# Strided cross-attention on Trainium2: three context pieces multiplied ahead of the first tokens, the second of them loaded at the first expert stage's end

## The reference

```python
Q = (hidden_states @ Wq.T + bq)          # 8 x 100 x 512, from the normalised x
K = (key_value_states @ Wk.T + bk)       # from the context
V = (key_value_states @ Wv.T + bv)
idx = jnp.arange(H)[:, None] + stride * jnp.arange(m)[None, :]   # head h: rows h, h+16, ...
scores = jnp.einsum('bhqd,bhkd->bhqk', Q, Kg) * scaling          # Kg, Vg: K, V at idx
out = softmax(scores) @ Vg, then @ Wo.T + bo
x = x + tanh(g_xattn[1]) * out
```

## Time and profile before

| | us |
|---|---|
| median of 3 runs | 2059.59 (2058.01 to 2061.52) |
| profiled execution | 2049.21 |
| its span, first to last instruction | 2047.5 |
| PE / DVE / ACT / POOL busy in the span | 1892.9 / 1043.0 / 801.4 / 641.8 |
| mean granted TensorE clock | 0.964 of full |

### The profile page before, as it was taken

One profiled execution on the slowest core, in us unless ns is written; L12 is line 12 of the kernel. 1 busy time (PEld: TensorE's weight loads), 2 busy tenths in 40 slices (PEclk: granted clock), 3 DMA queues, 4 the chain that ended last, 5 costly groups with the idle time before them and its releaser, 6 DMA issues. The chain is left out here.

```text
span 2047.5 us, 35305 instructions
## 1 busy us (share of the span) xinstructions
PE 1892.9 (92%) x12136; PEld 1542.4 (75%) x12136; DVE 1043.0 (51%) x2405; ACT 801.4 (39%) x1728; POOL 641.8 (31%) x522
## 2 busy tenths in 40 slices
PE   5799999999999999999589999999997876999994
PEld 3588788787878787878468888888875656999983
DVE  5616465565656565645553333233335755554564
ACT  3324243333434343433343334233313534555650
POOL 1220110302020202000045554355520204787872
PEclk9899999999999999999789999999998977999997
DMA  8730213122121112010333333133368034545546
GB/s 289 237 104 30 75 38 72 46 60 58 54 63 54 30 54 59 9 26 10 105 119 109 113 113 123 54 105 110 116 210 283 13 129 136 182 163 165 204 150 207
DMA packets 131587, 218.85 MB, mean 107 GB/s; under 512 B 46075, under 2 KB 50971, under 8 KB 130671
## 3 DMA queue, kind: packets, MB, share of 16 engines
q1 hardware_dynamic: 126431, 200.46, 30.6%
q0 software_dynamic: 5008, 16.48, 2.4%
HBM read 188.87 MB, written 28.04 MB: 106 GB/s over the span
## 5 line engine op out<-in xcount | busy, mean ns | idle before, releaser
L492 POOL TENSOR_TENSOR a_cols<-a_cols,a_moments_b 128x722 f32<-128x722 f32 x32 | 56.6, 1768 | 545.3 <-DMA a_moments_b<-a_moments_dram 545.3
L634 PE MATMUL a_kv_ps<-a_kvin_hi,a_wk_hi 128*128 128x512 f32 (+1 forms) x512 | 195.5, 382 | 0.0
L1098 PE MATMUL f_banks<-f_wab_hi,f_x_hi 128*128 x448 | 183.6, 410 | 2.6 <-DVE f_x_lo L1785 1.4
L635 PE MATMUL a_kv_ps<-a_kvin_lo,a_wk_hi 128*128 128x512 f32 (+1 forms) x512 | 179.7, 351 | 0.0
L636 PE MATMUL a_kv_ps<-a_kvin_hi,a_wk_lo 128*128 128x512 f32 (+1 forms) x512 | 179.6, 351 | 0.0
L1100 PE MATMUL f_banks<-f_wab_hi,f_x_lo 128*128 x448 | 176.3, 394 | 0.0
L1099 PE MATMUL f_banks<-f_wab_lo,f_x_hi 128*128 x448 | 175.8, 392 | 0.0
L568 ACT ACTIVATE a_probs<-a_probs,a_neg_max 100x822 f32<-100x822 f32 x128 | 125.9, 984 | 115.1 <-DVE a_neg_max L916 115.1
L1807 DVE TENSOR_TENSOR f_h_sb<-f_h_sb,f_banks 128x256 f32<-128x256 f32 x112 | 47.2, 421 | 239.9 <-ACT f_h_sb L1530 237.6
L634 PE MATMUL a_kv_ps<-a_wv_hi,a_kvin_hi 128*128 128x512 f32 (+1 forms) x384 | 157.0, 409 | 2.3 <-DVE a_k_lo L909 2.2
L1530 ACT ACTIVATE f_h_sb<-f_banks 128x256 f32<-128x256 f32 x112 | 43.1, 385 | 292.8 <-PE f_banks L1100 283.9
(11 more groups left out here) (419 smaller groups left out, 4786.1 us busy)
## 6 DMA issues: line engine op xcount, KB each, us to landing
f_raw<-f_pieces SPq DMA_DIRECT2D x94, 256.0 KB, 2.7
m_raw<-m_pieces SPq DMA_DIRECT2D x92, 256.0 KB, 2.9
f_wab_raw<-f_pieces SPq DMA_DIRECT2D x42, 512.0 KB, 5.9
m_wab_raw<-m_pieces SPq DMA_DIRECT2D x42, 512.0 KB, 6.0
a_cols<-ctx_cols SPq DMA_DIRECT2D x8, 1444.0 KB, 7.5
a_rows<-ctx SPq DMA_DIRECT2D x8, 1280.0 KB
ahead_piece<-g_ctx SPq DMA_DIRECT2D x2, 2880.0 KB, 20.7
a_moments_b<-a_moments_dram SPq DMA_DIRECT2D x7, 722.0 KB
```

The lines of the kernel that those rows point to most:

```text
L634: nc.tensor.matmul(out, hi_l, hi_r, start=first, stop=False)
L635: nc.tensor.matmul(out, hi_l, lo_r, start=False, stop=False)
L1098: nc.tensor.matmul(out, left_hi, right_hi, start=start, stop=False)
```

## The change

SP issues piece 1 right behind `load_stream`, at the first expert stage's end, and not behind y half 0; piece 2 takes piece 1's place in the attention's list, and piece 3 stands alone behind y half 1. PE multiplies pieces 0, 1 and 2 before the first tokens, and piece 3 between half(0) and tokens(4). The banks are dealt out in the new order. ACT's order follows: keys and values of 0, keys 1, deviations(0), values 1, keys 2, deviations(1), values 2, tokens 0 to 3, query weights, queries 0 to 3, deviations(2), keys and values 3, tokens 4 to 7, queries 4 to 7. DVE's and POOL's orders stay.

```diff
--- before.py
+++ after.py
@@ -1398,6 +1398,7 @@
                     ahead.load_values(sp)
                     ahead.load_piece(sp, 0)
                     handed.load_stream(sp)
+                    ahead.load_piece(sp, 1)
                 else:
                     sp.wait_ge(y_scattered, 16 * SLOTS)
             with sp.Else():
@@ -2083,9 +2085,9 @@
         ROUTED = 3
         GROUPS = ((0, 1, 2, 3), (4, 5), (6, 7))
         bank_use = {}
-        for kind, n in (("k", 0), ("v", 0), *(("x", b) for b in range(HB)), ("k", 1), ("v", 1), *(("q", m) for m in range(KD)),
-                        ("k", 2), ("v", 2), *(("x", b) for b in range(HB, B)), *(("q", m) for m in range(KD, 2 * KD)),
-                        ("k", 3), ("v", 3)):
+        for kind, n in (*((kind, c) for c in range(3) for kind in "kv"), *(("x", b) for b in range(HB)),
+                        *(("q", m) for m in range(KD)), ("k", 3), ("v", 3),
+                        *(("x", b) for b in range(HB, B)), *(("q", m) for m in range(KD, 2 * KD))):
             bank_use[kind, n] = len(bank_use)
         BANK_USES = len(bank_use) // 4
         assert len(bank_use) % 4 == 0
@@ -2107,10 +2109,9 @@
             sp.wait_ge(sums.tail_done, 1)
             sp.wait_ge(sums.scattered, 16 * sums.core)
             sums.load_half(sp, 0)
-            ahead.load_piece(sp, 1)
+            ahead.load_piece(sp, 2)
             sp.dma_start(wq_raw[:, :, :], wq_t).then_inc(wq_loaded, 16)
             sums.load_half(sp, 1)
-            ahead.load_piece(sp, 2)
             ahead.load_piece(sp, 3)
             sp.wait_ge(mid_done, B)
             sp.dma_start(wo_raw[:, :, :], wo_t).then_inc(wo_loaded, 16)
@@ -2181,24 +2182,26 @@
                                      scale=SCALE).then_inc(fill_free("q", n), 1)
 
             act.wait_ge(zero_k, 1)
+            act.wait_ge(const_done, 2)
             move_keys(0)
             move_values(0)
-            act.wait_ge(const_done, 2)
-            for g in range(2):
-                deviations(g)
-                for b in EQUAL[g]:
-                    move_tokens(b)
+            move_keys(1)
+            deviations(0)
+            move_values(1)
+            move_keys(2)
+            deviations(1)
+            move_values(2)
+            for b in range(HB):
+                move_tokens(b)
             act.wait_ge(wq_loaded, 16)
             for k in range(KD):
                 nc.scalar.activation(wq_hi[:, k, :], wq_raw[:, k, :], ACT.Copy).then_inc(wq_hi_done, 1)
-            move_keys(1)
-            move_values(1)
             act.wait_ge(q_bias_done, 1)
             for n in range(KD):
                 move_queries(n)
             deviations(2)
-            move_keys(2)
-            move_values(2)
+            move_keys(3)
+            move_values(3)
             for b in range(HB, B):
                 move_tokens(b)
             def high_output_weights(k):
@@ -2210,8 +2213,6 @@
                 move_queries(n)
                 if n >= KD + 2:
                     high_output_weights(n - KD - 2)
-            move_keys(3)
-            move_values(3)
             for k in range(2, KD):
                 high_output_weights(k)
             act.wait_ge(c_loaded, 32)
@@ -2310,18 +2311,17 @@
                 for n in range(KD * h, KD * h + KD):
                     queries(n)
 
-            context(0)
+            for c in range(3):
+                context(c)
             pe.wait_ge(const_done, 3)
             for b in range(HB):
                 tokens(b)
-            context(1)
             pe.wait_ge(wq_lo_done, KD)
             half(0)
-            context(2)
+            context(3)
             for b in range(HB, B):
                 tokens(b)
             half(1)
-            context(3)
 
             def element(b):
                 if b >= 4:
```

## The result

| us | before | changed |
|---|---|---|
| median, 20 runs of each | 2056.71 (2046.34 to 2061.98) | 2061.66 (2055.74 to 2067.89) |
| profiled execution | 2049.21 | 2055.74 |
| its span | 2047.5 | 2054.0 |
| PE / DVE / ACT / POOL busy | 1892.9 / 1043.0 / 801.4 / 641.8 | 1895.5 / 1046.0 / 801.9 / 642.3 |
| mean granted TensorE clock | 0.964 | 0.963 |

The ratio of the times, run against run, is 1.0025 (95% interval 1.0013 to 1.0037): the changed kernel is slower by about 5 us, a quarter of a per cent.

The account below looks back on a forecast made before the run. PE was taken as bound by waits for tokens, sequences, piece 2 and DVE, plus low-clock stretches. Half(0) at 1569.1 + 30.3 + 3.3 = 1602.7 against 1598.65, +4.0 on 2059.6: 2063.6 us, range 2057.0 to 2067.5.

Parts of the forecast that it names:

- Step 1: At the expert stage's end, piece 1's early transfer makes the last scatters wait, delaying SP's release by 4.0 us.
- the estimate by equal turns: For the scatters beside piece 1: queues sharing engines equally from 1525 on would make the delay nearer 3 us than 4.
- The room: Idle DMA engine time between 1526 and 1536, at share 0.65: 3.5 us of piece 1's 7.1 fit in.
- up to another microsecond of the room isn't usable: In SP's delay: the idle stretch's end lies behind the last scatter's data, so 3.6 us left over became 4.0.
- Step 2: At SP's wait for the scatters: everything behind moves by 4.0 us; piece 2 lands at 1556.5, not 1552.5.
- Step 3: In PE's gap: contexts 0 and 1 cost nothing, context(1) ending near 1544.5, with cover for 3 us of lateness.
- Step 4: From context(2) to half(0): its keys and ACT's order take 12.6 us; half(0) starts at 1569.1, 8.9 us later.
- Step 5: From half(0) to the softmax: 30.3 us against 38.5, so 8.2 saved, including the 2.0 wait for the piece.
- Step 6: TensorE clock in the halves: one low stretch of 1.65 us in half(0) and one in half(1), 3.3 in all.
- the scatters kept their time: Rival at the expert stage's end: POOL's packets go ahead of piece 1, delay 0, time 2059.6 us; chance 0.16.
- The clock didn't stay high: Judges a rival: smaller delay and contexts keeping the clock up through both halves, 3.3 us less, 2056.3; chance 0.10.
- The transfers slow each other: Rival: piece 1 mixed with scatters moves slower; delay near 10, time 2069.7, or halfway at 7, 2066.6; chance 0.15.

Follow-up runs that it names:

- e5: The changed kernel with piece 1 issued ahead of the stream's loads instead of behind them; single time 2058.95 us.
- e2: The changed kernel with piece 1 loaded where it was, behind y half 0, and the new order kept; ratio 1.0026 against before.
- e12: The kernel before with half of piece 1 loaded early, ahead of the stream, and 44, 8 and 8 added products in PE's waits; ratio 0.9987.
- e3: The changed kernel with context(2) behind half(0), context(3) behind half(1), and ACT's moves and transfers of pieces 2 and 3 as before; ratio 1.0020 against before.
- e6: The changed kernel with 36 added products, all to one column group, behind tokens(3); ratio 1.0125 against before.
- e9: The changed kernel with 16 added products, spread over four column groups, behind tokens(3); ratio 1.0018 against before.
- e11: e3 with piece 1 ahead of the stream, query weights' high parts earlier on ACT, low parts on POOL, and 16, 8, 8 added products; ratio 1.0009 against before.
- e10: e9 with 52 more added products ahead of context(2); ratio 1.0010 against before.
- e8: The kernel before with half of piece 1 loaded early, and 90, 20 and 18 added products ahead of tokens(0), tokens(2) and half(1); ratio 1.0323.

## Why the prediction was right, and where it wasn't

The forecast was 2063.6, +4.0 on the median it stood against. The change measured about +5, and +4.14 in the filling part. The sum's softmax at 1602.7 answers to 1604.89 - 2.10 = 1602.79 here. That closeness isn't all merit: two errors of opposite sign cancel. Half(0) came 1.4 later than forecast (53.76 for 52.4 behind the stream's issue), and what follows it took 1.3 less (32.3 for 33.6).

**Step 1, the delay of SP: sign right, size short, mechanism wrong.** Forecast 4.0, measured 5.4. The forecast let the scatters wait until piece 1 was through, and looked for no packets of POOL's queue until 1532. They came from 1528 on, 1526 by the clock of the trace before, and the trace has 1.83 MB of SP's beside 1.42 MB of theirs from 1532 to 1540. What the forecast had read from rows 5 holds while the stream's packets ran; beside piece 1's the scatters moved. The rule that the prediction held against itself, from the Trainium skill's "DMA: Bandwidth & Descriptors", section "Queues, rings and completion order", that the engines take turns between queues, fits the packets from 1528 on; it doesn't fit those from 1521 to 1528, nor those from 1523 to 1526 in e5 (98.0% is SP's). But the estimate by equal turns, nearer 3, was farther off than 4.0. The room was right (3.75 for 3.5); the term that failed is "up to another microsecond of the room isn't usable": the thin end cost about 2.

**Step 2, piece 2's landing.** Forecast +4.0, measured 41.47 behind the stream against 35.76 for that place: +5.7, step 1's error handed on.

**Step 3, contexts 0 and 1 in the gap: right.** Context(1) began at 1545.18 and PE stood idle for 10.09 us afterwards. Context(0) began 1.5 us later than before (19.24 against 17.76 behind the stream), at the low clock, its keys 4.87 for 2.63; the prediction had allowed for 3 us of cover. In e2 and e12, where SP was released in time, it began 17.77 and 18.00 behind the first issue; where SP was released late, at 18.9 to 19.4.

**Step 4, what context(2) holds up: right.** From its start to half(0)'s, 1560.31 to 1572.60, is 12.3 us, forecast 12.6; e3 shows the 8.0 us that the place costs, with the transfer and ACT's order that go with it, by taking all three away.

**Step 5, what is saved behind it: right.** No wait at context(3); from half(1)'s end at about 1600.7 to the softmax 4.2, forecast 4.3.

**Step 6, the clock: half right.** Half(0) had its low stretch (10.8 us for 8.8), as forecast. Half(1) didn't, and the 1.65 put there was too much. The evidence was one pair of transposes and idleness in one trace, and the experiments show that this pair goes either way, seven times low and four times full. So the term should have been a chance of about two in three on 1.6, not 1.65. In this execution it covered the 1.4 by which steps 1 and 2 had put half(0) too early. Over many runs it is a mean, which may be part of why the runs say +5 and the trace +4.1; that wasn't measured. The rule that transposes don't count as work ("TensorE: Matmul & The Clock Gate", section "Part 4: PE-mode transpose", of the Trainium skill) agrees with half(0) in the changed kernel, e2, e3 and e5; as 4 us of idleness stood beside the transposes there, these traces don't separate the two.

**The rivals.** With an early load the scatters kept their time, but for 0.4 us, only where half a piece went ahead of the stream (e12). The clock didn't stay high in half(0). "The transfers slow each other" began at 7: the measured 5.4 lies between it and the forecast, but not by its mechanism, as both queues together moved 402 GB/s.

## What to carry to other kernels

A transfer put ahead of work in an idle-looking queue is paid where the last transfer behind it ends: sum the idle share that it can fill, and add something for the thin end, where the engines' share falls while the last transfers trail in. Of two loads, the one whose packets fill the engines at half the rate should run where something else can run beside it. When a step is moved ahead of an in-order engine's short instructions, as 0.30 us of square root behind keys that wait for a piece, the wait moves to everyone behind them, so each engine's list has to be checked, not only the one with the gap. A clock state seen once behind a short idle pattern is a chance, not a term; products put right ahead of the work were followed by the full clock in every trace here, which is few.

## What the runs showed of the hardware, unexpected

- Products of 32 output columns that all go to one group of columns take 0.61 us each (e6, 22.0 us for 36); spread over four groups, 16 take 2.63 us (e9), 0.16 each.
- DVE's normalising pair took 2.75 us and not 1.00 while POOL ran a subtraction (e11, seen once).
- At a full share of the DMA engines the stream's 2 KB packets moved 209 GB/s and the piece's 5.8 KB packets 408; put ahead of the stream, the same piece released SP 2.6 us earlier (e5).
- Sixteen products that nobody reads, in idle time ahead of half(0), were followed by the full clock (e9, e10) where four kernels without them had a low stretch, and half(0) started no later in e9 (53.57 for 53.76). Ahead of half(1), where the clock went either way without them, eight or eighteen were followed by it too (e8, e11, e12).
- In e5 no packet of POOL's queue moved from 1523 to 1526, though a scatter was issued at 1522.31; from 1530 to 1536 both queues ran at equal shares. Why is open.
- Where the scatters ended late, context(0), which doesn't wait for them, began 1.2 to 1.6 us later. Why is open as well; the gap behind it hides it.
